# An adapter layer and a long convolution on one core: even weight sums from blocks loaded twice, A rows in a buffer of their own and split later, filter set-up later

## What is computed

```python
result = jnp.einsum('bsd,od->bso', x, base_weight) + base_bias
h = jnp.einsum('bsd,brd->bsr', x, lora_A_w[adapter_ids])
result = result + jnp.einsum('bsr,bor->bso', h, lora_B_w[adapter_ids])
...
dtA = A * dt[:, None]
Ct = Cc * (jnp.exp(dtA) - 1.0) / A
P = dtA[:, :, None] * jnp.arange(length)
K = 2.0 * jnp.einsum('hn,hnl->hl', Ct, jnp.exp(P)).real
y = irfft(rfft(u, n=2L) * rfft(K, n=2L))[..., :L] + u * D[:, None]
return y * mask[:, None, :]
```

## Time and profile before

| | us |
|---|---|
| median of 3 runs (1180.15 to 1187.92) | 1181.69 |
| profiled execution | 1188.34 |
| its span, first to last instruction | 1186.6 |
| PE busy (share of the span) | 1093.9 (92%) |
| DVE busy | 882.1 (74%) |
| ACT busy | 717.5 (60%) |
| POOL busy | 69.2 (6%) |
| mean granted PE clock | 0.958 of full |

### The profile page before, as it was taken

How to read it: one execution, slowest core, us unless ns; L and a number is a source line. 1 busy time by engine, 2 the same in 40 slices (tenths; PEclk the granted TensorE clock), 3 DMA queues, 4 the chain that set the end, 5 groups by cost and what they waited for, 6 DMA issues and landing times.

```text
span 1186.6 us, 21568 instructions
## 1 busy us (share of the span) xinstructions
PE 1093.9 (92%) x8088; PEld 1056.6 (89%) x8088; DVE 882.1 (74%) x1282; ACT 717.5 (60%) x1260; POOL 69.2 (6%) x93
## 2 busy tenths in 40 slices
PE   9386989899988999899898999899979999999998
PEld 8286889899988999899897999899968999999997
DVE  7985687676868676677866768687547888888886
ACT  4173444655555645546545646645449888888885
POOL 3631000000000000000000000000000000000000
PEclk9698989899989999899989999999989999999999
DMA  7155377767777777777776777778679779798783
GB/s 250 58 196 188 139 234 267 228 221 239 230 240 228 240 197 255 239 218 248 223 243 206 232 240 242 218 226 277 185 263 346 282 314 331 284 346 294 308 294 124
DMA packets 162587, 284.62 MB, mean 240 GB/s; under 512 B 10739, under 2 KB 125620, under 8 KB 149044
## 3 DMA queue, kind: packets, MB, share of 16 engines
q1 hardware_dynamic: 162484, 283.26, 70.8%
HBM read 193.96 MB, written 89.26 MB: 239 GB/s over the span
## 4 chain that ended last, share of the span: by engine, by line
PE 47%; SPq 15%; DVE 14%; DMA 10%; ACT 8%; issue 6%; POOL 0%; ACTq 0%; DVEq 0%
PE acc L1912 22%; PE acc L1754 14%; PE acc L1760 7%; SPq L431 5%; DVE x_lo L1052 5%; DMA x_scratch<-x_sb 5%; SPq L435 3%; SPq L470 2%; SPq L439 2%; PE acc L1947 2%; DMA a_raw<-lora_a 2%; DVE x_sb L1179 2%; ACT L830 1%; DVE t_lo L1052 1%; ACT L843 1%
## 5 line engine op out<-in xcount | busy, mean ns | idle before, releaser
L1052 DVE TENSOR_TENSOR t_lo<-t_raw,t_hi 128x1024 fp32r<-128x1024 f32 x63 | 77.1, 1224 | 153.2 <-ACT t_hi L671 152.8
L1754 PE MATMUL acc<-x_hi,w_pair 128*128 128x256 f32 x720 | 110.9, 314 | 57.2 <-ACT acc L671 49.6
L1754 PEld LDWEIGHTS acc<-x_hi,w_pair 128*128 128x128 f32 x720 | 103.3, 219 | 60.3 <-ACT acc L671 51.9
L1754 PE MATMUL acc<-t_hi,v_hi 128*128 128x256 f32 x512 | 124.6, 282 | 7.8 <-ACT x_sb L671 7.8
L1912 PE MATMUL acc<-u_hi,f_hi 128*128 128x512 f32 (+1 forms) x320 | 129.2, 404 | 0.0
L1754 PE MATMUL acc<-t_hi,v_lo 128*128 128x256 f32 x512 | 124.3, 281 | 0.0
L1754 PE MATMUL acc<-t_hi,w_pair 128*128 128x256 f32 x960 | 122.6, 279 | 0.8 <-ACT t_hi L671 0.7
L1912 PE MATMUL acc<-u_lo,f_hi 128*128 128x512 f32 (+1 forms) x320 | 118.5, 370 | 0.0
L1912 PE MATMUL acc<-u_hi,f_lo 128*128 128x512 f32 (+1 forms) x320 | 118.4, 370 | 0.0
L1754 PEld LDWEIGHTS acc<-t_hi,w_pair 128*128 128x128 f32 x960 | 116.8, 188 | 1.3 <-issue 1.3
L671 ACT ACTIVATE acc<-acc 128x512 f32<-128x512 f32 x93 | 52.9, 582 | 93.5 <-PE acc L1760 93.0
(11 more groups left out here) (219 smaller groups left out, 2771.4 us busy)
## 6 DMA issues: line engine op xcount, KB each, us to landing
w_pair<-weight_scratch SPq DMA_DIRECT2D x73, 1024.0 KB, 6.2
x_scratch<-x_sb SPq DMA_DIRECT2D x32, 1024.0 KB, 6.4
out<-out_sb SPq DMA_DIRECT2D x63, 512.0 KB, 4.6
x_raw<-x_t SPq DMA_DIRECT2D x15, 2048.0 KB, 7.8
u_raw<-x_scratch SPq DMA_DIRECT2D x14, 2048.0 KB, 12.4
wq_raw<-state_scratch SPq DMA_DIRECT2D x16, 1024.0 KB, 7.7
a_raw<-lora_a SPq DMA_DIRECT2D x128, 64.0 KB, 1.9
b_raw<-lora_b SPq DMA_DIRECT2D x128, 64.0 KB, 2.2
```

The source lines that it names most:

```text
L1052: return dve.tensor_tensor(dst, src, r32(hi), ALU.subtract)
L1754: pe.matmul(by_row(bank_part(bank, i)), w[:, k, i, :], hi[:, k, :, :], start=opens and i == 0 and k == 0 and s == 0, stop=False, skip_grou ...
```

## The change

- The even sums are computed by DVE from raw blocks: `load_blocks` loads the four even weight blocks a second time, after the last plain tile, into slots 2 and 3 and the place of s4_even; DVE forms S1, S2, S4 behind v's last split (`even_sums`), S3 in group 1 (`even_sum_3`), and adds the identity to S1 and S3. ACT makes the hi and DVE the lo parts, S2 first, then S4, S3, S1. S4 and S1 go straight into slots 0 and 1, are used from there in group 1, and are stored from there. POOL's ten sums and four lo parts go, and t4(0) no longer waits for them.
- On SyncE's queue x of group 1 is issued after the blocks and the stores of A11 and A12.
- a_raw gets a place of its own; split_a(g+1) moves on ACT behind the second out_11 and on DVE behind T1 lo; the A loads no longer wait for the odd x1 store, nor out_11(1) for the A rows.
- Both exponentials of the filter set-up become one series on [128, 2, 64]; the set-up begins at the last place of group 1 and goes on in group 2, whose exponents are stored there; the first unit moves from group 1 to group 2's last place, and groups 5, 8 and 11 have a fourth place. `turn_exponents` on PE moves into group 2, behind p6.
- In the last group take_p5(0) and out_12(0) move ahead of the first filter and u splits, and the last unit's store ahead of A22's load.
- The mask and two work tiles share places with others to make room.

```diff
-    a_raw = place("a_raw", [P, G, NT, rank], F32, at=x1_at + X1_BYTES + N * 4)
+    a_raw = place("a_raw", [P, G, NT, rank], F32)
...
     def stream_loads(n):
-        return 16 * (n // 2)
+        return 16 * (n // 2 - 1)
...
+    UNIT_PLACES = [(2, PER_GROUP - 1)] + [(g, i) for g in range(3, LAST)
+                                          for i in range(PER_GROUP + (1 if g in (5, 8, 11) else 0))]
...
+            def load_blocks():
+                sp.wait_ge(m_plain, 1)
+                sp.wait_ge(st_ws[STREAM.index(A22)], 16)
+                for dst, r, c in ((w_raw[:, 2, 0, :, :, :], 1, 0), (w_raw[:, 3, 0, :, :, :], 1, 1),
+                                  (w_raw[:, 2, 1, :, :, :], 0, 0), (s4_even[:, :, :, :], 0, 1)):
+                    sp.dma_start(dst.rearrange("p k i n -> p (k i n)"), w_even[r, c]).then_inc(ld_e, 16)
...
             load_filter_inputs()
-            load_x(1)
+            load_blocks()
             store_plain(A11, 0)
             store_plain(A12, 1)
+            load_x(1)
             store_x1(0, 0)
...
-                if g == 1:
-                    sp.wait_ge(c_elo, 3)
-                    store_sum(S4)
                 load_ws(g, S4)
-                if g == 1:
-                    sp.wait_ge(c_elo, 4)
-                    store_sum(S1)
                 if g < LAST:
                     rows = [adapter_of(g + 1, i) for i in range(G)]
                     sp.wait_ge(c_alo, 2 * (g + 1))
-                    sp.wait_ge(st_x1[1], 16 * g)
                     for i, row in enumerate(rows):
                         load_a(i, row)
                 load_ws(g, S1)
-                if g == 2:
+                if g == 1:
+                    store_sum(S4, 0)
+                if g == 3:
                     load_zb(0)
                 filter_stores(g, 0)
                 if g < LAST:
                     load_x(g + 1)
+                else:
+                    store_unit(ALL_UNITS - 1)
                 load_ws(g, A22)
+                if g == 1:
+                    store_sum(S1, 1)
                 filter_stores(g, 1)
-                if g == 1:
+                if g == 2:
                     store_exponents()
...
@@ ACT, in a group @@
                 split_t(g, "T3")
-                if g < LAST:
-                    split_a(g + 1)
+                if g == 1:
+                    split_even(S1)
                 filter_step(g, 0)
                 seed_c(0, g)
                 seed_c(1, g)
                 out_11(0, g)
                 split_t(g, "T1")
                 out_11(1, g)
+                if g < LAST:
+                    split_a(g + 1)
                 filter_step(g, 1)
...
@@ DVE @@
+            def even_sums():
+                a11, a21, a22 = w_raw[:, 2, 1, :, :, :], w_raw[:, 2, 0, :, :, :], w_raw[:, 3, 0, :, :, :]
+                s1, s2, s4 = s1_even[:, :, :, :], w_raw[:, KEPT[S2], 1, :, :, :], s4_even[:, :, :, :]
+                dve.wait_ge(ld_e, 16 * 4)
+                even_sum(s1, a21, a22, ALU.add, 1)
+                even_sum(s2, s1, a11, ALU.subtract, 2)
+                even_sum(s4, s4, s2, ALU.subtract, 3)
+                even_residual(s1, 4)
...
             split_v(A22)
+            even_sums()
             split_t(0, "T4")
...
@@ DVE, in a group @@
                 t2(g)
+                if g == 1:
+                    split_even(S2)
                 split_t(g, "T2")
+                if g == 1:
+                    even_sum_3()
                 filter_step(g, 0)
                 keep_own(g)
                 split_h(g)
                 split_b(g)
+                if g == 1:
+                    split_even(S4)
+                    split_even(S3)
                 split_t(g, "T3")
+                if g == 1:
+                    split_even(S1)
+                t4(g)
+                split_t(g, "T1")
                 if g < LAST:
                     split_a(g + 1)
-                t4(g)
-                split_t(g, "T1")
                 filter_step(g, 1)
...
@@ POOL @@
-            even_sums()
-            for n, j in enumerate((S2, S3, S4, S1)):
-                even_low(n, j)
```

More of the change, by code:

```diff
@@ L104, in lora_s4d_kernel @@
     tiny.update({n: place("k_" + n, [P, heads], F32) for n in passing_names})
-    pow2_i = place("pow2_i", [P, heads], I32)
+    pair = {}
+    for names in paired_names:
+        pair[names[0]] = place("k_both_" + names[0], [P, 2, heads], F32)
+        tiny.update({n: pair[names[0]][:, i, :] for i, n in enumerate(names)})
+    pow2_i = place("pow2_i", [P, 2, heads], I32)
     work_end = cursor[0]
@@ L164, in lora_s4d_kernel @@
     v_shape = [P, HALF, QT, P]
[L165 to L168, removed]
+    s1_even = place("s1_even", v_shape, F32, at=zb_at)
+    s4_even = place("s4_even", v_shape, F32, at=ge_at)
     zeros = place("zeros", [heads, KPAD], F32, at=t_hi_at)
@@ L196, in lora_s4d_kernel @@
     out_sb = [place(f"out_sb{i}", [P, 2, n_groups, W8], F32) for i in range(OUT_EARLY)]
+    mask = place("mask", [P, 2, n_groups, HALF, G], U8)
     assert cursor[0] <= ge_at + 3072
@@ L846, in filter_step @@
             def filter_step(g, place):
-                if g == 1 and place == 1:
+                if g == 1 and place == 2:
                     filter_pre()
@@ L1111, in split_v, with even_sum, even_residual, even_sum_3 @@
                 minus_hi(v_lo[:, j, :, :, :], v_raw[:, j, :, :, :], v_hi[:, j, :, :, :]).then_inc(c_vlo, 1)
+            def even_sum(out, a, b, op, count):
+                dve.tensor_tensor(out, a, b, op).then_inc(c_esum, 1)
+                dve.wait_ge(c_esum, count)
+            def even_residual(t, count):
+                add_identity(t[:, 0, 0, :])
+                add_identity(t[:, 2, 1, :]).then_inc(c_esum, 1)
+                dve.wait_ge(c_esum, count)
+            def even_sums():
[6 more added lines that the diff above has]
+                even_residual(s1, 4)
+            def even_sum_3():
+                s3 = w_raw[:, KEPT[S3], 1, :, :, :]
+                even_sum(s3, s3, w_raw[:, 2, 0, :, :, :], ALU.subtract, 5)
+                even_residual(s3, 6)
+            def split_even(j):
+                dve.wait_ge(c_ehi, EVEN_ORDER.index(j) + 1)
+                slot, raw = {S2: (KEPT[S2], w_raw[:, KEPT[S2], 1, :, :, :]), S3: (KEPT[S3], w_raw[:, KEPT[S3], 1, :, :, :]),
+                             S4: (0, s4_even[:, :, :, :]), S1: (1, s1_even[:, :, :, :])}[j]
+                minus_hi(w_pair[:, slot, 1, :, :, :], raw, w_pair[:, slot, 0, :, :, :]).then_inc(c_elo, 1)
             def split_x(g, t):
@@ L1422, in filter_step @@
             def filter_step(g, place):
[L1423 to L1425 removed]
+                if g == 1 and place == 2:
                     filter_exponents()
[L1427 removed]
+                if g == 2 and place == 0:
+                    filter_quotients()
+                if g == 2 and place == 1:
                     keep_exponents()
[L1429 removed]
                     filter_weights()
@@ L1432, in filter_step @@
                     make_diag()
-                    dve.wait_ge(st_ws[STREAM.index(S1)], 32)
+                if g == 3 and place == 0:
+                    dve.wait_ge(c_elo, len(EVEN_ORDER))
                 if g == LAST and place == 0:
```

176 lines of the change are left out of this document (73 added, 103 removed).

## The result

The changed kernel takes 1111.31 us (median of 4 runs, 1109.44 to 1114.91) against 1181.70 for the kernel before in the same comparison (4 runs): a ratio of 0.940, 95% interval [0.936, 0.944]. Predicted were 1117.0 us and a range of 1084 to 1152. The profiled execution took 1110.4 us, its span is 1108.7 and the granted clock 0.991 of full (0.958 before).

A forecast was written before the change was run, and what follows sets the result against it. PE was taken as the bound, 92% busy, idle some 93 us, mostly waiting for ACT's seed copies. Terms: 15.5 + 17.0 + 60.3 - 35 + 6.7 = 64.5 off 1188.3, 1123.8, scaled to 1117 us; range 1084 to 1152.

The forecast's parts named there:

- Next late is A22's load: Group 1: A22's load, behind the stored S4, lands just before its use; if it doesn't, 3 us.
- The estimate of 617.4 us without late work: Groups 2 to 14: 8 groups with filter matmuls at 47.8 us and 5 without at 47.0, against 677.7 before.
- 35 given back: Groups 2 to 14: losses of 2 + 5 + 24 + 4 us, subtracted from the 60.3 us to be had.
- in groups 4, 7, 10, 13 ... 2 us: Groups 3, 4, 7, 10, 13: seed_c still behind h, T3 and, in the last four, an ACT unit; 2 us lost.
- for what I don't see 3.5: Groups 2 to 14: an allowance of 3.5 us for unseen losses, beside 0.5 us for the set-up.
- four times 1.2, 5 us: Groups 5, 8, 11, 14: an ACT unit in the second place follows a 3.7 us DVE unit; 5 us lost.
- Three times: 24: Fourth filter unit ending groups 5, 8, 11: late seed, b's low part and partly slow restarts cost 8 us each, 24 together.
- the seed stays late: Rival, groups: h, T3 and the filter unit still end after PE wants seed_c; 36 us stay, 1153 us; chance 0.16.
- all hidden: Rival, groups 2 to 14: the 35 us given back don't occur, 1083 us; chance 0.15.
- 3 us of waiting before the second stage: Last group: out_21 and the even parts still behind u, 3 us of waiting expected; 6.7 us gained.
- that rival: Transfers bound the groups: only start, group 1 and the end gain, 39 us, 1143 us; chance 0.08.
- the slower one: Rival, later groups: transfers set the group period, under 202 GB/s, making the kernel slower than before; 1209 us at 195; chance 0.02.

The follow-up runs named there:

- dummy adds: The changed kernel with ten unneeded 128x1024 additions on POOL from about 20 us on: 1123.46 us.
- The later split alone: The kernel before with only the A rows' own buffer, the x1 store wait dropped and the A split behind the second out_11: 1130.36 us.
- the restored wait: The changed kernel with the A loads waiting again for the odd x1 store of the group before: 1111.29 us.
- the early split: The changed kernel with the A split back ahead of the first filter place on ACT, DVE the like, own buffer kept: 1135.38 us.

## Why the prediction was right, point by point

**Start** (15.5 predicted, 17.9 measured). "DVE would then be ready for h about 1.5 us before ACT has it: 16.5 us earlier at the first product of v" held: 38.61 us where it was 55.09. The 0.5 us for the low part of T4 came as 0.4. What I had wrong is x of group 1: I left PE's old wait of 3.3 us in place and added 0.5, as if nothing of it was POOL's, and it fell by 2.2, to 1.16 (POOL's low parts had stood beside x_lo). x was there at 62.69, between the 60 and 69 of my bounds. The dummy adds show the cause for 11.0 of the 17.9 us.

**Group 1** (17.0, 18.5). Both waits went and nothing took their place. "Next late is A22's load": it went out at 91.29 and PE did not wait. The later split alone got 3.7 of it.

**Groups 2 to 14** (25.3, 32.9). The estimate of 617.4 us without late work carried the sum, and 27.4 of the "35 given back" were there. It was itself 2 us too long: a group without waits takes 47.6 us with filter matmuls and 46.9 without, 615.3 in all, so 29.4 us were lost to late work. The steps "in groups 4, 7, 10, 13 ... 2 us" (0 found) and "for what I don't see 3.5" with "0.5" for the set-up (0.7 found, all in group 2) were too large; "four times 1.2, 5 us" came as four waits of 1.0 for T4's high part and 0.2 each behind them, 5.0. "Three times: 24" came out at 23.8 (groups 6, 9 and 12 take 55.0, 54.8 and 54.7), but by other terms, so that the close sum is in part luck: the seed waits are 4.39 each, not 2.9. DVE's chain took 16.9 us where I counted 17.6; yet PE wanted the seed 12.5 us after DVE's start, not 14.7, as the third place began 2.9 and not 5.3 us before PE's next group (301.60 against 304.51). The waits for b are 0.8 to 1.45 where I had 2.6, and what the slow restarts cost is 2.9, 2.0 and 1.9 us (the group's busy time over 46.9), not far from the 2.5. The wait for the stored blocks, in the sum with 7.6 us, did not occur.

"It is not the shared buffer that makes A late but the reads, and ACT's order that makes it matter": the restored wait (no cost, 5.5 us from S4's issue to the A loads with and without it) and the early split (24 us) bear it out. The rival *the seed stays late* is out: with the later split groups 2 to 14 have no seed wait but the three behind the fourth places. The rival *all hidden* (1083) was refused with "the fourth unit's chain has no slack that I can find". True at the group's end, where the change has it; with the fourth place behind the second one inside a group, and the units shifted accordingly, nearly all of the same forty units' work is hidden, and the kernel takes 1091.46.

**Last group** (6.7, 8.6). The store's place and the order were both named; "3 us of waiting before the second stage" was 1.2. What I had wrong is their weights. I gave PE's 7.8 us wait and its restart to the order; undone alone, with the store early, the order brings back a wait of 2.4 and 2.6 us in all, while the store's place carries 5.1.

**Transfers.** 245 GB/s in the groups and 357 in the best slice: neither that rival nor the slower one came near.

**Luck.** Against the profiled execution the terms fell 13.4 us short (64.5 against 77.9), and the forecast still came within 5.7 us of the median, because 6.3 us were taken off as the distance of before's profiled execution from its median, while the changed kernel's profiled execution lay at its own. By the medians the gain is 70.4 us, so how much of the 13.4 was an error of the terms, and how much the slow execution that they were read from, stays open.

## What to carry to other kernels

A wait of the bound engine is seldom cured where it is: find the instruction ahead of its releaser, in that engine's order, whose result is wanted latest, and move it behind; moving the split of the A rows was worth some 50 us here (51.6 by the medians of the kernel with this part alone), dropping the loads' wait for the old buffer nothing. Count a piece of work by the place it gets and by what each in-order queue then stands for: against a fourth place in the middle of a group, one at the group's end cost 2.5 us more where its unit had no ACT work and 6 us more where it had. Keep sums that read on-chip memory off POOL while DVE is the bound.

## What the runs showed of the hardware that I had not expected

- Under POOL's adds (2.48 us each) each of DVE's two-input instructions is longer by 0.8 to 1.7 us, so the small ones suffer most for their size: 2.91 us for 128x1024 (1.22 alone), 1.49 for 128x512 (0.65), 1.04 for 128x128 (0.26). POOL's memsets of the same tile, 1.01 us each, cost DVE nothing.
- After three waits of the same 4.39 us the next 16 matmuls took 3.78, 3.14 and 3.57 us; in a row without a wait such 16 take 2.05, and after waits of 1.03 us 2.11. The granted clock was at its lower level from 317.1 to 323.9 us around the first (PEclk 0.50), and for 3.4 us only around the others (from 470.7 and from 620.9): the groups lost 2.9 us to it and 2.0 and 1.9. A restart has no fixed price; behind the waits of 1.03 us the clock did not fall.
- The u loads, issued 7.7 us later, took 3.0 us less to land: an earlier issue was worth less than the time by which it was earlier. What they shared the DMA engines with was not told apart.
